# Order of TensorE inside an attention step: the products moved in front of the second pair's scores

## The chip, the cores and the metric

One core of a Trainium2 chip runs the whole kernel in one launch. The metric is the time on the device in microseconds (us), median of three runs. All inputs and outputs are 32-bit floats in device memory.

## The reference

An AdaLN block over x of shape (2, 1024, 256): causal attention with 32 query heads and 8 key/value heads of width 8, then a feed-forward layer with 16 routed experts (top 4) and a shared one. Cut to what matters here, the attention:

```python
q = (h @ wq) ; k = (h @ wk) ; v = (h @ wv)          # 32 query heads, 8 key/value heads, width 8
att = einsum('bhqd,bhkd->bhqk', q, k) / sqrt(8)
att = where(mask, -inf, att) ; att = softmax(att)    # causal, 1024 x 1024 per head
y = einsum('bhqk,bhkd->bhqd', att, v)
x = x + ga * (y @ wo)
```

## The kernel before

The kernel has a prologue (modulation, layer norm, projections), the attention core, a post stage (output projection, second norm, router) and the expert layer. The change is in the attention core alone.

**Groups and steps.** The core runs over 16 groups (2 batches times 8 key/value heads). A group holds four query heads, two "pairs of heads" hh = 0 and 1, and the two heads of a pair lie in the upper and lower 64 rows of the array (hp = 0, 1). The causal triangle of a group is cut into 12 steps (STEPS): queries in two halves of 512, keys in chunks c of 128. Steps 0 to 3 are the first half, steps 4 to 11 the second. Queries above the diagonal are left out, so the width of a step is 512, 384, 256, 128 in steps 0 to 3, 512 in steps 4 to 8, and 384, 256, 128 in steps 9 to 11. Below, step 8.6 is step 6 of group 8.

**The softmax needs the row maximum first.** While group g is worked on, TensorE also computes the scores of a later group in the other orientation (queries on partitions) and VectorE reduces them to maxima. These are the 12 wide units (`wide(n)`, into two PSUM banks that only they use, reduced by L709) and 12 narrow units (`narrow(n)`, one bank, reduced by L716) per group; step s of group g does unit n = 12(g+1) + 6 + s (AHEAD = 6). A next wide unit waits for `wide_free`, the end of the reduction before, a narrow one for `narrow_free`. The wide unit of step 6 is the first that reads the stacks (operands) of group g+2, and waits for their load (`stack_in`).

**One step.** `scores(group, s, hh)` writes two banks per pair of heads with keys on partitions (L665) and signals `st_full`; it may not start before ScalarE has read those banks for the step before (`p_full`). ScalarE takes one exponential per pair (L608, `probs<-psum`). `product(group, s)` (L679, `psum<-probs,v_aug`) multiplies the exponentials of all four heads with the values, four matmuls in four 32-column strips of the array (the profile counts eight, since a 32-bit float product runs as two passes), and adds into one bank, `sum_bank`. It runs LAG = 2 steps after its scores. On diagonal chunks GpSimd masks the exponentials first (L585).

**The sum bank.** Products 0 to 3 accumulate the first half, products 4 to 11 the second. When a half is complete, ScalarE copies the bank to `y_sb` (L600), queued behind both exponentials of step 5 (first half) and of step 1 of the next group (second half). The first product of a half waits for that copy:

```python
if c == 0 and 2 * group + half:
    pe.wait_ge(y_done, 2 * group + half)
```

With the lag of 2 these waiting products are product(4), issued in step 6, and product(0), issued in step 2.

**SyncE.** One queue issues all transfers. At the start of a group it waits until all scores of the group before are done, then issues the 16 loads of the stacks of group g+2 and, in groups 1 to 3, the three loads of an expert's raw weights:

```python
if 1 <= group < GROUPS - 2:
    sp.wait_ge(st_full, 2 * NSTEP * group)
    load_stacks(sp, group + 2)
```

In groups 0 to 3 ScalarE turns those raw weights into `w_hi` (L616), queued between the exponentials of step 3 and of step 4.

All engines run their instructions in the order written; only semaphores tie them together.

Of the kernel before, what the change touches and what calls it, by code (L numbers as in the profile page):

```python
# [31 lines left out]
GROUPS = B * NKV  # L32
# [34 lines left out]
NPAIR = len(WIDE)  # L67
# [19 lines left out]
def block_kernel(nc, x_in, wq_in, wk_in, wv_in, wo_in, wr_in, we1_in, we3_in, we2_in,  # L87
# [13 lines left out]
    with whole:  # L101
# [414 lines left out]
        with nc.Block() as block:  # L516
# [102 lines left out]
            @block.tensor  # L619
            def _(pe):  # L620
                def wide(n):

                    group = n // NPAIR
                    w, (h0, h1), tiles, chunk, _, diagonal = WIDE[n % NPAIR]
                    segments = [(hh, i) for hh in range(h0, h1) for i in range(*tiles)]
                    buf = group % NBUF
                    if n % NPAIR == 0:
                        pe.wait_ge(stack_in[buf], LOADS * (group // NBUF + 1))
                    if n:
                        pe.wait_ge(wide_free, n)  # L630
                    for k, (hh, i) in enumerate(segments):
                        key = i * P if w == P else chunk * P
                        for hp in range(2):
                            rows = slice(64 * hp, 64 * hp + 64)
                            if not diagonal:
                                keys = ku[buf][rows, key:key + w]
                            elif i % 4 == 0:
                                keys = kx[buf][rows, (i + 3) * P:(i + 4) * P]
                            else:
                                keys = (kx, kx, ky)[i % 4 - 1][buf][rows, key:key + w]  # L640
                            last = pe.matmul(bank[wide_bank + hp][:, k * w:(k + 1) * w], qs[buf][rows, hh, i * P:(i + 1) * P],  # L641
                                             keys, start=(k == 0), stop=(k == len(segments) - 1), skip_group_check=True)
                    last.then_inc(wide_full, 1)

                def narrow(n):

                    group = n // NPAIR
                    hp, hh, i = NARROW[n % NPAIR]
                    buf, rows = group % NBUF, slice(64 * hp, 64 * hp + 64)
                    if n:  # L650
                        pe.wait_ge(narrow_free, n)
                    pe.matmul(bank[narrow_bank][:], qs[buf][rows, hh, i * P:(i + 1) * P], ku[buf][rows, 0:TT],  # L652
                              start=True, stop=True).then_inc(narrow_full, 1)

                def scores(group, s, hh):

                    half, c, off = STEPS[s]
                    buf = group % NBUF
                    if s == 0 and hh == 0:
                        pe.wait_ge(row_in[buf], 32 * (group // NBUF + 1))  # L660
                    if 2 * NSTEP * group + 2 * s + hh > 1:
                        pe.wait_ge(p_full, 2 * NSTEP * group + 2 * s + hh - 1)
                    for hp in range(2):
                        rows = slice(64 * hp, 64 * hp + 64)
                        last = pe.matmul(bank[2 * hh + hp][:, off:TT], ks[buf][rows, c * P:(c + 1) * P],  # L665
                                         qs[buf][rows, hh, half * TT + off:(half + 1) * TT],
                                         start=True, stop=True)
                    last.then_inc(st_full, 1)

                def product(group, s):  # L670

                    half, c, off = STEPS[s]
                    if c == 0 and 2 * group + half:
                        pe.wait_ge(y_done, 2 * group + half)
                    pe.wait_ge(p_full, 2 * NSTEP * group + 2 * s + 2)
                    if c >= half * (TC // 2):
                        pe.wait_ge(p_masked, NDIAG * group + c + 1)
                    for h in range(REP):
                        last = pe.matmul(bank[sum_bank][32 * h:32 * h + 32, off:TT], v_aug[:, group, c, :],  # L679
                                         probs[:, s % (LAG + 1), h, off:TT], start=(c == 0),  # L680
                                         stop=(c == (TC // 2, TC)[half] - 1), skip_group_check=True)
                    last.then_inc(pv_done, 1)

                pe.wait_ge(parts_set, 1 + 2 * NBUF)
                for n in range(NPAIR + AHEAD):
                    wide(n)
                    narrow(n)
                for group in range(GROUPS):
                    for s in range(NSTEP):
                        n = NPAIR * (group + 1) + AHEAD + s  # L690
                        scores(group, s, 0)
                        if n < NPAIR * GROUPS:
                            wide(n)
                        scores(group, s, 1)
                        if n < NPAIR * GROUPS:
                            narrow(n)
                        if s >= LAG:
                            product(group, s - LAG)
                        elif group:
                            product(group - 1, s - LAG + NSTEP)  # L700
                for s in range(NSTEP - LAG, NSTEP):
                    product(GROUPS - 1, s)

            @block.vector
            def _(dve):
                def wide(n):
                    w, (h0, h1), tiles, _, slot, _ = WIDE[n % NPAIR]
                    dve.wait_ge(wide_full, n + 1)
                    dve.tensor_reduce(out=max_parts[:, :, h0:h1, slice(*tiles), slot],  # L709
                                      in_=psum[:, wide_bank:wide_bank + 2, :].rearrange("p a (s w) -> p (a s) w", w=w),  # L710
                                      axis=AX.X, op=ALU.max).then_inc(wide_free, 1)
# [438 lines left out]
```

## Time and profile before

| | us |
|---|---|
| median of three runs | 965.73 (963.19 to 966.53) |
| time of the profiled execution | 965.71 |
| its span | 963.8 |
| attention core (first scores to last product) | about 138.0 to 549 of the span |

Busy shares of the span: TensorE's matmuls 87%, its weight loads 56%, VectorE 68%, ScalarE 45%, GpSimd 21%. These are averages over stages with different limits; a matmul's end is modelled, so that matmuls that follow closely look like an engine that is always busy. Times below are in us from the span's start; a group of the core takes 24.1 us where nothing else disturbs it (groups 4 to 13), 30 to 32 us in groups 0 to 3, and about 22 us in the last two.

### The profile page before, as it was taken

The page shows a single profiled execution, that of the slowest core. Times are in us where ns is not written, and L with a number is a line of the kernel's source. Part 1 is how long each engine was busy: PE and PEld are TensorE (multiplying, and loading weights), DVE is VectorE, ACT ScalarE, POOL GpSimd, SP SyncE. Part 2 cuts the span into 40 slices and gives each one's busy share as a digit, 9 for nine tenths or more (in the row PEclk, how much of TensorE's full clock was granted, in tenths as well). Part 3 has the DMA queues.
Part 4 walks back from the last instruction along what each step waited for, and adds up shares of the span by engine and source line. Part 5 has one row for each costly group of instructions (what it writes and reads, how often), then busy time and mean ns, then how long its engine had stood idle before and what let it go on. Part 6 is the DMA issues. An engine that isn't in the chain of part 4 may idle for free. (4 is left out here: it accounts for less than half of the span.)

```text
span 963.8 us, 15004 instructions
## 1 busy us (share of the span) xinstructions
PE 835.8 (87%) x5472; PEld 539.3 (56%) x5472; DVE 659.6 (68%) x1053; ACT 433.0 (45%) x629; POOL 204.3 (21%) x261
## 2 busy tenths in 40 slices
PE   0791579879799999999999677699999999999996
PEld 0550334334344444444443257488888888888885
DVE  0751887678699999999994144777656666665665
ACT  3121016666677777777778704222222222222221
POOL 8600002122122222222222123782000000000000
PEclk9896558788899999999999976699999999999999
DMA  5069300443234343444430160440000000000000
GB/s 181 1 174 230 59 19 24 99 95 82 53 93 92 92 93 92 93 93 92 92 81 26 45 185 0 126 121 17 1 22 0 0 22 0 0 0 22 0 0 22
DMA packets 50627, 61.15 MB, mean 63 GB/s; under 512 B 12624, under 2 KB 37200, under 8 KB 49488
## 3 DMA queue, kind: packets, MB, share of 16 engines
q1 hardware_dynamic: 50576, 60.47, 25.6%
q8 instruction: 32, 0.52, 0.2%
q14 instruction: 19, 0.16, 0.1%
HBM read 42.35 MB, written 17.56 MB: 62 GB/s over the span
## 5 line engine op out<-in xcount | busy, mean ns | idle before, releaser
L608 ACT ACTIVATE probs<-psum 128x1024 f32<-128x1024 f32 (+3 forms) x384 | 289.0, 817 | 134.3 <-PE psum L665 132.3
L709 DVE TENSOR_REDUCE max_parts<-psum 128x8 f32<-128x1024 f32 (+2 forms) x192 | 235.0, 1224 | 58.6 <-PE psum L641 54.3
L665 PE MATMUL psum<-qs,ks 64*128 64x512 f32 (+3 forms) x768 | 162.4, 420 | 18.3 <-ACT probs L608 18.1
L679 PE MATMUL psum<-probs,v_aug 128*32 128x512 f32 (+3 forms) x1536 | 168.7, 513 | 0.3 <-POOL probs L585 0.2
L665 PEld LDWEIGHTS psum<-qs,ks 64*128 64x128 f32 x768 | 75.1, 192 | 154.5 <-ACT probs L608 132.8
L992 ACT ACTIVATE mid<-psum 128x512 f32<-128x512 f32 x80 | 47.9, 599 | 243.6 <-PE psum L1015 243.6
L585 POOL TENSOR_SCALAR_AFFINE_SELECT probs<-probs 128x512 f32<-128x512 f32 x128 | 81.4, 636 | 238.0 <-ACT probs L608 238.0
L716 DVE TENSOR_REDUCE max_parts<-psum 128x1 f32<-128x512 f32 x192 | 130.8, 681 | 0.0
L1103 DVE TENSOR_TENSOR mid<-mid,psum 128x512 f32<-128x512 f32 x80 | 54.9, 688 | 104.7 <-ACT mid L992 104.2
L1094 DVE SCALAR_TENSOR_TENSOR acc<-psum,cw,acc 128x256 f32<-128x256 f32 x240 | 99.2, 475 | 0.0
L652 PE MATMUL psum<-ku,qs 64*128 64x512 f32 x192 | 91.5, 476 | 0.0
L1015 PE MATMUL psum<-h_hi,wl_hi 128*128 x256 | 79.6, 392 | 0.0
L1015 PE MATMUL psum<-h_hi,wl_lo 128*128 x256 | 79.2, 390 | 0.0
L1015 PE MATMUL psum<-h_lo,wl_hi 128*128 x256 | 79.0, 390 | 0.0
L974 POOL TENSOR_TENSOR fin<-fin,gate 128x256 f32<-128x256 f32 x4 | 3.0, 738 | 294.3 <-DVE fin L1112 294.3
L679 PEld LDWEIGHTS psum<-probs,v_aug 128*32 128x32 f32 x1536 | 30.8, 109 | 58.2 <-issue 42.0
L641 PE MATMUL psum<-kx,qs 64*128 64x128 f32 (+1 forms) x384 | 38.9, 312 | 28.1 <-DVE ks L734 24.2
L1082 DVE TENSOR_TENSOR g_lo<-mid,g_hi 128x512 fp32r<-128x512 f32 x80 | 59.9, 749 | 1.0 <-ACT g_hi L988 0.9
L988 ACT ACTIVATE g_hi<-mid 128x512 fp32r<-128x512 f32 x80 | 50.0, 625 | 9.2 <-DVE mid L1103 7.8
L1015 PEld LDWEIGHTS psum<-h_hi,wl_lo 128*128 128x128 f32 x256 | 48.1, 188 | 10.6
L1015 PEld LDWEIGHTS psum<-h_lo,wl_hi 128*128 128x128 f32 x256 | 48.1, 188 | 10.4
L641 PEld LDWEIGHTS psum<-kx,qs 64*128 64x128 f32 x384 | 31.8, 212 | 36.4 <-DVE ks L734 24.3
(132 smaller groups left out, 1004.4 us busy)
## 6 DMA issues: line engine op xcount, KB each, us to landing
qs<-q_parts SPq DMA_DIRECT2D x64, 128.0 KB
y_sums<-y_sb SPq DMA_DIRECT2D x32, 256.0 KB, 3.0
wl_raw<-in_L_ffn_we_dram SPq DMA_DIRECT2D x36, 128.0 KB, 2.2
ks<-k_parts SPq DMA_DIRECT2D x32, 128.0 KB
ku<-k_parts SPq DMA_DIRECT2D x32, 128.0 KB
ky<-k_parts SPq DMA_DIRECT2D x32, 128.0 KB
kx<-k_parts SPq DMA_DIRECT2D x32, 96.0 KB
x_sb<-in_L_attn_x_dram SPq DMA_DIRECT2D x4, 512.0 KB, 7.6
```

The costliest lines, as they stand in the source:

```text
L585: pool.affine_select(out=tile, in_=tile, compare_op=ALU.is_ge, fill=0.0, base=0, pattern=[[0, REP], [1, P]], channel_multiplier=-1).then_i ...
L608: act.activation(probs[:, s % (LAG + 1), 2 * hh:2 * hh + 2, off:TT], psum[:, 2 * hh:2 * hh + 2, off:TT], ACT.Exp, scale=SCALE).then_inc(p_ ...
L641: last = pe.matmul(bank[wide_bank + hp][:, k * w:(k + 1) * w], qs[buf][rows, hh, i * P:(i + 1) * P], keys, start=(k == 0), stop=(k == len( ...
L652: pe.matmul(bank[narrow_bank][:], qs[buf][rows, hh, i * P:(i + 1) * P], ku[buf][rows, 0:TT], start=True, stop=True).then_inc(narrow_full, 1)
L665: last = pe.matmul(bank[2 * hh + hp][:, off:TT], ks[buf][rows, c * P:(c + 1) * P], qs[buf][rows, hh, half * TT + off:(half + 1) * TT], sta ...
L679: last = pe.matmul(bank[sum_bank][32 * h:32 * h + 32, off:TT], v_aug[:, group, c, :], probs[:, s % (LAG + 1), h, off:TT], start=(c == 0), ...
L709: dve.tensor_reduce(out=max_parts[:, :, h0:h1, slice(*tiles), slot], in_=psum[:, wide_bank:wide_bank + 2, :].rearrange("p a (s w) -> p (a ...
L716: dve.tensor_reduce(out=max_parts[:, hp, hh, i:i + 1, 1], in_=bank[narrow_bank][:], axis=AX.X, op=ALU.max).then_inc(narrow_free, 1)
L1015: last = pe.matmul(bank[2 * m + e % 2][:], w[:, col:col + H], h[:, c, bass.ds(at, TT)], start=(n == 0), stop=(n == 5))
L1082: dve.tensor_tensor(out=g_lo[:, e % 2, :], in0=mid[:, e % 2, :], in1=g_hi[:, e % 2, :].bitcast(F32), op=ALU.subtract).then_inc(glo_done, 1)
L1094: last = dve.scalar_tensor_tensor(out=acc[:, j, :], in0=y, scalar=weight, in1=acc[:, j, :], op0=ALU.mult, op1=ALU.add)
L1103: dve.tensor_tensor(out=m, in0=m, in1=bank[2 + e % 2][:], op=ALU.mult).then_inc(mult_done, 1)
```

## The change

The product of step s - 2 is issued directly behind the wide unit, ahead of the scores of the second pair of heads and of the narrow unit. No instruction is added or removed, and no wait is changed; no other engine's program changes.

```diff
@@ -691,13 +691,13 @@
                         scores(group, s, 0)
                         if n < NPAIR * GROUPS:
                             wide(n)
-                        scores(group, s, 1)
-                        if n < NPAIR * GROUPS:
-                            narrow(n)
                         if s >= LAG:
                             product(group, s - LAG)
                         elif group:
                             product(group - 1, s - LAG + NSTEP)
+                        scores(group, s, 1)
+                        if n < NPAIR * GROUPS:
+                            narrow(n)
```

TensorE's order in steps 5 and 6 of a group (the first rows are step 5). L665 are scores, L641 the wide unit, L652 the narrow one, L679 the product; the product of 128 columns is the last one of the first half, the product of 512 columns behind it the first of the second half. Before:

```order
L665 MATMUL psum<-qs,ks 128x512 x2
L641 MATMUL psum<-ky,qs 128x512 x2
L665 MATMUL psum<-qs,ks 128x512 x2
L652 MATMUL psum<-ku,qs 128x512
L679 MATMUL psum<-probs,v_aug 32x128 x4
L665 MATMUL psum<-qs,ks 128x512 x2
L641 MATMUL psum<-kx,qs 128x128 x8
L665 MATMUL psum<-qs,ks 128x512 x2
L652 MATMUL psum<-ku,qs 128x512
L679 MATMUL psum<-probs,v_aug 32x512 x4
```

and after:

```order
L665 MATMUL psum<-qs,ks 128x512 x2
L641 MATMUL psum<-ky,qs 128x512 x2
L679 MATMUL psum<-probs,v_aug 32x128 x4
L665 MATMUL psum<-qs,ks 128x512 x2
L652 MATMUL psum<-ku,qs 128x512
L665 MATMUL psum<-qs,ks 128x512 x2
L641 MATMUL psum<-kx,qs 128x128 x8
L679 MATMUL psum<-probs,v_aug 32x512 x4
L665 MATMUL psum<-qs,ks 128x512 x2
L652 MATMUL psum<-ku,qs 128x512
```

In step 6 the product that waits for the copy of the sum bank now stands ahead of the second pair's scores, and in step 5 the product that completes the bank too.

TensorE's order in step 11 and at the start of the next group, where the last scores of a group release SyncE's loads. Before:

```order
L665 MATMUL psum<-qs,ks 128x128 x2
L641 MATMUL psum<-ku,qs 128x512 x2
L665 MATMUL psum<-qs,ks 128x128 x2
L652 MATMUL psum<-ku,qs 128x512
L679 MATMUL psum<-probs,v_aug 32x384 x4
L665 MATMUL psum<-qs,ks 128x512 x2
```

and after:

```order
L665 MATMUL psum<-qs,ks 128x128 x2
L641 MATMUL psum<-ku,qs 128x512 x2
L679 MATMUL psum<-probs,v_aug 32x384 x4
L665 MATMUL psum<-qs,ks 128x128 x2
L652 MATMUL psum<-ku,qs 128x512
L665 MATMUL psum<-qs,ks 128x512 x2
```

A product of 384 columns now runs before the last scores of the group, where it ran behind them.

## Rows read from the trace of the kernel before

**Rows 1.** Page, part 1: busy us, share of the span, instructions of each engine.

```profile
PE 835.8 (87%) x5472; PEld 539.3 (56%) x5472; DVE 659.6 (68%) x1053; ACT 433.0 (45%) x629; POOL 204.3 (21%) x261
```

**Rows 2.** Windows: length, busy of PE, PEld, DVE, ACT, POOL, granted clock, DMA share, GB/s.

```profile
168.12:200.08 31.96, 27.69 (x204) 12.26 (x200) 22.33 (x27) 19.84 (x27) 7.36 (x12) 0.84 0.36 83
212.00:222.00 10.00, 7.18 (x38) 3.32 (x40) 4.11 (x6) 7.21 (x8) 2.28 (x3) 0.50 0.11 37
359.73:383.83 24.10, 24.00 (x205) 10.62 (x202) 22.22 (x27) 18.75 (x26) 5.55 (x11) 1.00 0.39 93
```

**Rows 3.** Timeline of steps 8.4 to 8.7: start, length, engine, line, operation.

```profile
367.45 0.49 PE L665 MATMUL psum<-qs,ks 64*128 64x512 f32 x2
...
368.04 1.94 ACT L608 ACTIVATE probs<-psum 128x1024 f32<-128x1024 f32 x2 [1.16 <-PE psum L665]
...
368.74 0.64 PE L679 MATMUL psum<-probs,v_aug 128*32 128x256 f32 x8
...
370.70 0.42 PE L679 MATMUL psum<-probs,v_aug 128*32 128x128 f32 x8
...
371.46 0.66 PE L641 MATMUL psum<-kx,qs 64*128 64x128 f32 x8
371.74 0.60 ACT L600 ACTIVATE y_sb<-psum 128x512 f32<-128x512 f32 x1
371.93 0.48 PE L665 MATMUL psum<-qs,ks 64*128 64x512 f32 x2
...
372.57 1.06 PE L679 MATMUL psum<-probs,v_aug 128*32 128x512 f32 x8
...
373.56 0.50 PE L665 MATMUL psum<-qs,ks 64*128 64x512 f32 x2
```

**Rows 4.** Timeline of steps 8.7 and 8.8, TensorE.

```profile
374.23 0.50 PE L665 MATMUL psum<-qs,ks 64*128 64x512 f32 x2
...
375.89 0.50 PE L665 MATMUL psum<-qs,ks 64*128 64x512 f32 x2
376.22 0.40 PE L641 MATMUL psum<-kx,qs 64*128 64x256 f32 x4
376.46 0.40 PE L665 MATMUL psum<-qs,ks 64*128 64x512 f32 x2
...
376.70 0.39 PE L652 MATMUL psum<-ku,qs 64*128 64x512 f32 x1
...
377.02 1.06 PE L679 MATMUL psum<-probs,v_aug 128*32 128x512 f32 x8
```

**Rows 5.** Waits in groups 4 to 13: who waited for whom, us in total, times, longest.

```profile
PEld psum L652 <- DVE max_parts L716: 8.7, 40, 0.3
...
PEld psum L641 <- DMA kx<-k_parts: 0.5, 2, 0.4
```

**Rows 6.** Timeline of steps 8.1 and 8.2, the other copy and its product.

```profile
363.53 0.63 ACT L600 ACTIVATE y_sb<-psum 128x512 f32<-128x512 f32 x1
...
364.78 1.07 PE L679 MATMUL psum<-probs,v_aug 128*32 128x512 f32 x8
```

**Rows 7.** Timeline of steps 14.6 and 14.7, without wide and narrow units.

```profile
516.34 0.60 ACT L600 ACTIVATE y_sb<-psum 128x512 f32<-128x512 f32 x1
...
516.99 1.06 PE L679 MATMUL psum<-probs,v_aug 128*32 128x512 f32 x8
...
518.83 0.49 PE L665 MATMUL psum<-qs,ks 64*128 64x512 f32 x2 [0.34 <-ACT probs L608]
519.25 0.64 PE L679 MATMUL psum<-probs,v_aug 128*32 128x512 f32 x4
```

**Rows 8.** Timeline of group 2 (its first scores start at 200.08).

```profile
199.00 0.77 SPq L188 DMA_DIRECT2D qs<-q_parts  x2
...
213.01 0.84 ACT L616 ACTIVATE w_hi<-w_raw 128x768 fp32r<-128x768 f32 x1 [5.75 <-DMA w_raw<-in_L_ffn_we_dram]
...
214.82 0.80 PE L665 MATMUL psum<-qs,ks 64*128 64x512 f32 x2 [5.06 <-ACT probs L608]
```

## The prediction

> **What bounds the kernel now.** I read the page first: TensorE's matmuls cover 87% of the span, more than any other engine [rows 1]. Since modelled ends hide short waits, I then cut the core into windows, one group each. An undisturbed group, such as group 8, takes 24.10 us, with TensorE busy for 24.00, VectorE for 22.22 and ScalarE for 18.75, all at full clock (1.00, the 2.4 GHz level) [rows 2]. So TensorE and VectorE are both close to their limit and ScalarE has slack on average. Groups 1 to 3 take about 32 us (group 1: 31.96) at a mean clock of 0.84 [rows 2]; what they wait for is in the timeline of group 2: ScalarE stands 5.75 us before `w_hi`, for the raw weights of an expert, and TensorE stands 5.06 us behind the exponential queued after it [rows 8]. Behind that gap the window 212 to 222 has a granted clock of 0.50, the 1.2 GHz level [rows 2].
>
> Inside a group the timeline shows what a step is made of. In step 8.8 nothing waits: scores to wide unit 376.22 - 375.89 = 0.33, wide to second scores 0.24, those to the narrow unit 0.24, narrow to product 0.32 [rows 4]; a product of 512 columns holds TensorE for 373.56 - 372.57 = 0.99 until the next scores start [rows 3]. The sum is 2.12 us. Step 8.7 is longer, 375.89 - 373.56 = 2.33, and 0.10 of it shows in wide to second scores: the latter start 0.67 behind the first scores (374.23) where 8.8 needs 0.57 [rows 3, 4]. They wait for the exponential of step 8.6. So ScalarE, idle on average, is the limit around steps 4 to 7 of each group, where all widths are 512 and the copy of the sum bank comes between.
>
> **The change part by part.** No instruction is added. TensorE's sum per step is the same if the two new neighbours cost what the old ones did. Wide to product: the rows have narrow to product at 0.32 [rows 4] and, without a wide unit between, a pair of scores to product at 519.25 - 518.83 = 0.42 [rows 7], the scores having waited; the lower bound is pair to pair, 0.24 [rows 4]. I take 0.32. Narrow to scores: I take 0.24, what pair to narrow costs; the upper bound is the 0.32 before a product. So 0.32 + 0.24 replaces 0.24 + 0.32, and the order is neutral by itself. What changes is who is ready when.
>
> *The second pair's scores come later*, by the length of the product. For 512 columns the timeline gives 1.06 with the modelled end and 0.99 to the next start; with the same 0.07 off, 256 columns take 0.64 - 0.07 = 0.57 and 128 take 0.42 - 0.07 = 0.35 [rows 3], and 384, halfway between 256 and 512, 0.78. *The product comes earlier*, ahead of scores and narrow unit. Its two waits for the copy of the sum bank are where both meet.
>
> Walk through steps 8.4 to 8.7, from the same start, 367.45. ScalarE's exponentials of 512 columns follow each other every 0.92 (two take 1.94, the second starting about 0.1 before the first ends) [rows 3].
> - Step 4: wide 367.45 + 0.33 = 367.78, product 368.10, second scores 368.10 + 0.57 = 368.67, complete 0.49 later at 369.16. The second exponential can start at 369.18; in the trace it started at 368.04 + 0.92 = 368.96. ScalarE is 0.22 late.
> - Step 5: scores 368.67 + 0.24 + 0.24 = 369.15, wide 369.49, product(3) 369.81, second scores 370.25, once the exponential of step 4 has ended at 370.20. Exponentials at 370.10 and 371.02, each 0.92 behind the former, the copy 371.94 to 372.54, where the trace has 371.74 to 372.34 [rows 3].
> - Step 6: the first scores wait for the first exponential of step 5, which ends at 371.12: 371.17. Eight small wide matmuls start later behind scores than two large ones, and I take 0.41: wide unit 371.58. The product would be ready 0.47 later (wide to scores, 371.93 - 371.46 [rows 3]), plus 0.08 as the difference of product to scores: 372.13. It waits for the copy, 372.54 + 0.05 = 372.59: **0.46 us of wait on TensorE**, with the second scores and the narrow unit queued behind it. They start at 373.58, where the trace has 371.93; the next step starts at 373.58 + 0.24 + 0.24 = 374.06 in place of 373.56: **+0.50**.
> - Step 7 then needs 2.13 and not 2.33, because its second scores no longer wait: **-0.19**.
>
> The same meeting at steps 1 and 2 is milder, and this walk is coarser. The copy runs 363.53 to 364.16 and product(0) starts 364.78 [rows 6]. With the second scores of step 1 pushed back by 0.35 less the wait they had, the copy ends near 364.47, product(0) starts at 364.52, the narrow unit follows at 364.52 + 1.0 + 0.12, and step 3 starts near 365.9 in place of 365.78 (364.78 + 1.00): **+0.15**. On the other side the narrow units wait for their bank: 8.7 us of idle weight-load queue in 40 waits, 0.87 us a group, of which only the part in steps bound by TensorE comes back [rows 5]. With the product ahead of it the narrow unit finds its bank free; I count the one wait of about 0.1 in step 11, **-0.1**. An undisturbed group becomes 0.50 - 0.19 + 0.15 - 0.1 = 0.36 us longer.
>
> *VectorE* gets the narrow unit later: wide to narrow becomes 0.32 + 1.0 + 0.24 = 1.56 in place of 0.48, and its wide reduction is done 1.14 after its start, so it idles ahead of the narrow one and no longer ahead of the wide one. The next wide unit is complete 0.24 + 0.33 + 0.40 - 0.39 = 0.58 behind the narrow one, while the narrow reduction takes 0.68: 0.1 late, which nobody waits for. Cost 0.
>
> *SyncE* is moved too. Its loads are released by the last scores of a group. In the trace the first load goes out at 199.00, 1.08 ahead of the next group's start [rows 8]. Behind a product of 384 columns (0.78), they complete about 0.2 ahead of it. Everything on that queue starts 0.9 later in its group. In groups 1 to 3 the raw weights are the bound: `w_hi` starts 213.01 - 200.08 = 12.93 into group 2, and all of step 5 hangs on it [rows 8]. So each becomes **+0.9** longer, less the 0.1 of step 11: 0.8. The waits for the copy cost nothing there, the first hidden under the stall of 5.06, the second because at the 0.50 clock wide unit and product are slower than the copy. From group 4 on only the stacks are loaded, and they arrive barely in time: in two groups of ten the wide unit of step 6 already waited, 0.5 us together [rows 5]. If that wait grows, it falls ahead of product(4), which waits 0.46 anyway, so I count 0 and keep 0.3 per group for the upper end.
>
> *The last two groups* have no wide unit and ScalarE runs without a pause. In step 14.6 product(4) starts at 516.99, as soon as the copy has ended (516.94) [rows 7]. Now the second scores stand behind it: 517.99, complete 518.48; their exponential would have followed the copy and one exponential, 516.84 + 0.92 = 517.76. That is +0.74 on the engine that bounds this stretch, and again in group 15; with about 0.25 for each of the two other places: **+2.0**.
>
> **Sum.** Groups 4 to 13: 10 x 0.36 = 3.6. Groups 1 to 3: 3 x 0.8 = 2.4. Group 0: 0.2. Groups 14 and 15: 2.0. Together +8.2 on the profiled execution's 965.71, which is the median of the runs (965.73) within 0.02: **974 us**. The post stage and the experts follow unchanged.
>
> **The rivals.**
> 1. *The product drains more behind a pair of matmuls* (slower still). Wide to product costs the 0.42 of the pair in rows 7 and not 0.32. Seven steps a group (2, 6 to 11) have no other limit, so 0.7 x about 13 = +9 more: 983. For it: the only row of a pair ahead of a product. Against it: those scores had waited, and step 8.7, where wide to second scores took 0.34 (0.67 less 0.33) after a wait, shows that a start that waited costs about 0.1 by itself [rows 4]. The Trainium skill, TensorEngine Tiling (Array Packing), Key Properties, says that a change of tiling mode drains the array. By that rule the change from 64-row to 32-column tiles costs the same twice a step in both orders, and only what is drained differs; the 0.32 behind one narrow matmul agrees with a drain but no row shows the wide one. Chance 0.17.
> 2. *No change.* Wide to product costs only 0.24, as between pairs. Then 7 x 0.08 = 0.56 a group comes back, 14 x 0.56 = 7.8, and the sum ends at +0.4: 966. Against it: every product in the trace starts at least 0.3 behind what precedes it. Chance 0.12.
> 3. *Faster: the copy is not what product(4) waits for.* The point that decides is 0.46 us: if the sum bank's copy ends before 372.13 on the clock of step 8.6, the +0.50 and +0.15 vanish, and what stays is the relief of second scores and narrow units, between -0.29 and -(0.19 + 0.87) a group. With -0.4, near the small end, over 13 groups and +2.4 for groups 1 to 3: -2.8, 963. For it: product(3) is out 0.89 earlier (370.70 to 369.81), so its own end never delays the copy. Against it: the copy is queued behind two exponentials that cannot be earlier. Chance 0.08.
> 4. *The forecast*, both kinds of copy wait and the later release of SyncE: 974, its own range 970 to 979. Chance 0.63.
>
> **How the numbers follow.** What a measurement of this kernel can tell from no change is about 0.3%, 2.9 us. Cases 1 and 4 are slower (0.80), case 2 within it and, with a small share of the edges, 0.12; case 3 faster, 0.08. The range runs from 967, between cases 2 and 4, to 984, past case 1, where it takes in 0.3 a group for the stacks. About 0.1 is left out on either side, nearly all of it below.
>
> **What would show it.** In the changed profile: an undisturbed group of 24.4 to 24.6 us; in the waits, product L679 held by `y_sb` L600 in every group for about 0.5; in steps 4 and 5 the second exponential later, and step 7 at 2.13; `w_hi` starting 13.8 us into groups 1 to 3; step 14.6 with product at about 517 and second scores at 518. It would be wrong if wide to product is far from 0.32, if the start that waits adds its own 0.1 behind a late product, or if the later release makes the wide unit of step 6 wait longer than the copy does.

## The result and the profile after

The changed kernel takes 978.78 us (978.27 to 981.78, 4 runs) against 964.46 us (962.42 to 966.53, 4 runs) of the kernel before: a ratio of 1.0155, 95% interval 1.0122 to 1.0188. It is slower by 1.2 to 1.9%. The forecast was slower, 974, with a range of 967 to 984. The sign and the place are right; the size is off. Between the two medians lie 14.3 us where I had summed 8.2.

First the windows of the changed kernel, groups 1, 2, 3, 8, 14, 15 and two short stretches (columns as in [rows 2]):

```profile
166.64:199.68 33.04, 27.94 (x202) 12.97 (x204) 22.61 (x27) 20.08 (x27) 7.37 (x11) 0.85 0.34 80
199.68:233.74 34.06, 27.95 (x204) 12.96 (x204) 22.60 (x27) 20.06 (x27) 7.37 (x11) 0.80 0.39 77
233.74:265.72 31.98, 26.88 (x202) 12.80 (x204) 22.50 (x27) 20.07 (x27) 7.38 (x11) 0.84 0.35 82
365.40:390.32 24.92, 23.81 (x202) 11.08 (x204) 22.32 (x27) 19.23 (x26) 5.56 (x10) 1.00 0.37 89
514.86:538.54 23.68, 21.70 (x175) 8.62 (x176) 12.60 (x16) 19.12 (x26) 5.27 (x10) 1.00 0.08 26
538.54:563.49 24.95, 20.86 (x162) 6.71 (x160) 1.75 (x1) 19.21 (x27) 6.02 (x10) 0.93 0.10 33
543.20:546.60 3.40, 3.40 (x20) 0.75 (x17) 0.00 (x0) 1.16 (x3) 0.40 (x2) 0.54 0.21 77
214.00:225.00 11.00, 9.20 (x50) 4.71 (x50) 5.27 (x7) 8.04 (x9) 2.28 (x3) 0.50 0.10 30
```

The undisturbed group went from 24.10 [rows 2] to 24.92 us, while TensorE's busy time in it went down, 24.00 to 23.81: it does the same work and waits more. All of the loss is in the attention core. The first scores start at 137.76 (before 138.04) and the last product ends at 563.49 (before 549.44), and what follows takes 413.6 us (before 414.4).

The waits in groups 4 to 13, the counterpart of [rows 5]:

```profile
DVE max_parts L716 <- PE psum L652: 21.8, 50, 0.8
PEld psum L641 <- DVE max_parts L709: 18.5, 60, 0.4
...
PEld psum L679 <- ACT y_sb L600: 9.5, 19, 0.7
...
PE psum L679 <- ACT y_sb L600: 6.0, 18, 0.5
PEld psum L641 <- DMA kx<-k_parts: 2.2, 6, 0.6
```

The product now waits for the copy of the sum bank, 0.5 at most on the matmul side, as forecast. Two further lines are larger than I gave them credit for: VectorE stands before the narrow reduction (21.8 us in 50 waits), and the wide unit stands for the end of the wide reduction (60 waits, six in each of ten groups).

Steps 8.3 to 8.6 of the changed kernel, the counterpart of [rows 3]:

```profile
372.82 1.22 DVE L709 TENSOR_REDUCE max_parts<-psum 128x4 f32<-128x1024 f32 x1
...
374.10 0.50 PE L641 MATMUL psum<-ky,qs 64*128 64x512 f32 x2
...
374.53 0.64 PE L679 MATMUL psum<-probs,v_aug 128*32 128x256 f32 x8
...
375.64 2.85 ACT L608 ACTIVATE probs<-psum 128x1024 f32<-128x1024 f32 x3 [0.44 <-PE psum L665]
...
377.63 0.50 PE L665 MATMUL psum<-qs,ks 64*128 64x512 f32 x2 [0.18 <-ACT probs L608]
...
377.98 0.56 PE L641 MATMUL psum<-kx,qs 64*128 64x128 f32 x8
378.37 0.61 ACT L600 ACTIVATE y_sb<-psum 128x512 f32<-128x512 f32 x1
...
379.04 1.06 PE L679 MATMUL psum<-probs,v_aug 128*32 128x512 f32 x8 [0.51 <-ACT y_sb L600]
...
380.04 0.50 PE L665 MATMUL psum<-qs,ks 64*128 64x512 f32 x2
```

Read upwards from the product at 379.04: it idled 0.51 for the copy (378.37 + 0.61 = 378.98). The copy followed three exponentials, the second of step 4 and both of step 5, that started at 375.64 after ScalarE had stood 0.44 for scores. Those were late because the wide unit of step 4 started only at 374.10: it waited for the wide reduction of step 3, which ran from 372.82 to 374.04. So one delay feeds the next, from VectorE through ScalarE to the product. Where the delay at VectorE comes from, and what it is worth, is taken up behind the experiments.

### The profile page after: what moved, and what is told of

It reads as the page before. It is cut to its first block and busy times, and to the rows that moved or that the text cites. A ratio compares the mean times of both kernels' runs of the same rounds, so it can differ in the third digit from the quotient of the medians.

```text
span 977.1 us, 15004 instructions
## 1 busy us (share of the span) xinstructions
PE 835.9 (86%) x5472; PEld 546.0 (56%) x5472; DVE 660.3 (68%) x1053; ACT 439.5 (45%) x629; POOL 204.7 (21%) x261
## 5 line engine op out<-in xcount | busy, mean ns | idle before, releaser
L608 ACT ACTIVATE probs<-psum 128x1024 f32<-128x1024 f32 (+3 forms) x384 | 295.8, 811 | 143.2 <-PE psum L665 143.0
L709 DVE TENSOR_REDUCE max_parts<-psum 128x8 f32<-128x1024 f32 (+2 forms) x192 | 234.2, 1220 | 26.0 <-PE psum L641 24.7
L665 PE MATMUL psum<-qs,ks 64*128 64x512 f32 (+3 forms) x768 | 171.5, 421 | 19.4 <-ACT probs L608 18.6
L679 PE MATMUL psum<-probs,v_aug 128*32 128x512 f32 (+3 forms) x1536 | 171.2, 519 | 11.1 <-ACT y_sb L600 10.3
L665 PEld LDWEIGHTS psum<-qs,ks 64*128 64x128 f32 x768 | 82.9, 192 | 163.1 <-ACT probs L608 139.5
L652 PE MATMUL psum<-ku,qs 64*128 64x512 f32 x192 | 86.1, 448 | 0.0
L641 PE MATMUL psum<-kx,qs 64*128 64x128 f32 (+1 forms) x384 | 44.5, 310 | 28.3 <-DVE ks L734 23.9
L679 PEld LDWEIGHTS psum<-probs,v_aug 128*32 128x32 f32 x1536 | 30.8, 109 | 51.0 <-issue 23.7
L641 PEld LDWEIGHTS psum<-kx,qs 64*128 64x128 f32 x384 | 37.6, 211 | 37.9 <-DVE ks L734 24.1
```

What stands on the lines that cost most here:

```text
L608: act.activation(probs[:, s % (LAG + 1), 2 * hh:2 * hh + 2, off:TT], psum[:, 2 * hh:2 * hh + 2, off:TT], ACT.Exp, scale=SCALE).then_inc(p_ ...
```

## The experiments

The theories at the outset:
- *Copy*: the product that waits for the copy of the sum bank holds up the second scores (and what follows from that).
- *VectorE*: the late narrow unit costs by itself, through VectorE and the wide bank.
- *SyncE*: the last scores of a group release the loads later.

All runs were compared with the kernel before on the same chip. "Group" means an undisturbed one of groups 4 to 13.

**1. Only the narrow unit behind the product.**

```diff
-                        if n < NPAIR * GROUPS:
-                            narrow(n)
                         if s >= LAG:
                             product(group, s - LAG)
                         elif group:
                             product(group - 1, s - LAG + NSTEP)
+                        if n < NPAIR * GROUPS:
+                            narrow(n)
```

> Order of a step: first scores, wide unit, second scores, product, narrow unit. Only the narrow unit is behind the product; the second scores stand where they stood before the change. If the waits for the copy of the sum bank are the whole loss (copy theory), nothing stands behind them but the narrow unit: an undisturbed group stays near 24.1 us, the kernel within 2 us of before. If VectorE's late narrow reductions, which then hold the wide bank, are a part of it (VectorE theory), a group takes 24.4 us or more and the kernel is 4 to 7 us slower than before. SyncE's release is as before in both, so groups 1 to 3 keep their 31.3 to 32 us.

Measured: 964.81 us, ratio 0.9997 (0.9978 to 1.0016), a group of 24.07 us. The wide unit waits for VectorE here too (21.6 us in 60 waits, more than in the changed kernel), but a late narrow unit alone costs nothing; the VectorE theory falls as a cause of its own. Groups 1 to 3 take 31.0, 32.5 and 31.6 us, two of them outside the 31.3 to 32 expected though SyncE's release is as before, so half a microsecond in a single one of these groups says little.

**2. Only the second scores behind the product.**

```diff
                             wide(n)
-                        scores(group, s, 1)
                         if n < NPAIR * GROUPS:
                             narrow(n)
                         if s >= LAG:
                             product(group, s - LAG)
                         elif group:
                             product(group - 1, s - LAG + NSTEP)
+                        scores(group, s, 1)
```

> Order of a step: first scores, wide unit, narrow unit, product, second scores. Only the second scores are behind the product. Copy theory: the product still waits for the copy ahead of the second scores, so nearly the whole loss stays, a group of 24.7 to 25 us and 976 to 980 us in all. VectorE theory: the narrow unit is early, VectorE has no gap, and at least 0.3 us a group comes back against the changed kernel, 24.6 us or less, near 973 us. SyncE's loads are released even later, so groups 1 to 3 are no shorter than in the changed kernel.

Measured: 989.03 us, ratio 1.0233 (1.0214 to 1.0253), a group of 25.5 us, 0.6 more than in the changed kernel. The expectation of the VectorE theory is missed by 0.9 us a group, but that of the copy theory is missed as well, by 0.5 us a group and 9 us in all. With the narrow unit early, the second scores start even later (in step 8.8 1.90 behind the first ones, in the changed kernel 1.72). Most of the extra 0.6 lies in steps 4 and 8 to 11, and not in the two steps of the copy; why each of those is longer isn't shown. The run rules out that an early narrow unit repairs the loss, and no more.

**3. The old order in the two steps of the copy.** A flag chooses, per step, where the product stands; here and in runs 4, 6, 7 and 8 only its condition differs:

```diff
+                        early = s not in (LAG, TC // 2 + LAG)
+                        if early:
+                            late_product()
                         scores(group, s, 1)
                         if n < NPAIR * GROUPS:
                             narrow(n)
+                        if not early:
+                            late_product()
```

> The changed order in all steps but 2 and 6, the two whose product waits for the copy; those keep the order of before. Copy theory: the waits of product L679 for y_sb vanish, a group takes 24.1 to 24.3 us, the last two groups 22.6 each, and what is left over before is the later release of SyncE in groups 1 to 3 (about 3 us): 967 to 970 us. VectorE theory: the narrow unit is still late in ten of twelve steps, so a group keeps at least 24.5 us and the kernel 972 us or more.

Measured: 973.12 us, ratio 1.0073 (1.0044 to 1.0102). About half of the loss is gone, but the groups are unequal, 24.25 to 25.01 us. The waits tell why (groups 4 to 13):

```profile
PEld psum L641 <- DMA kx<-k_parts: 5.6, 9, 1.0
...
PE psum L641 <- DMA kx<-k_parts: 3.0, 7, 0.7
```

With the copy's wait gone, the wide unit of step 6 waits for the stacks, up to 1.0 us. In the changed kernel that wait had been hidden ahead of the copy's. The copy theory's numbers (24.1 to 24.3 us a group, 967 to 970) are both missed. VectorE's total (972 or more) is met, its 24.5 us a group is not met in three of the ten groups. Run 3 alone can't separate them, runs 5 and 11 do.

**4. The old order in step 11 alone** (condition `early = s != NSTEP - 1`).

> The changed order in all steps but 11, which keeps the order of before, so that the last scores of a group, and with them SyncE's loads, are not behind a product. SyncE theory (0.9 us in each of groups 1 to 3 comes from the later release): raw weights land about 13 us into the group and not 14, groups 1 to 3 are 0.7 to 1 us shorter each than in the changed kernel, 976 us in all, and a group from 4 on stays at 24.9. If the release doesn't matter: groups 1 to 3 as in the changed kernel (33.0, 34.1, 32.0), 978 to 979 us.

Measured: 981.54 us, ratio 1.0156 (1.0137 to 1.0175). Groups 1 to 3 take 30.7, 31.1 and 32.6 us in place of 33.0, 34.1 and 32.0, together 4.7 less, and `w_hi` starts 12.60 us into group 2 in place of 14.30: the later release is real. The kernel gets no faster and misses its 976, since a group takes 25.22 us, 0.3 more, and group 15 takes 27.4 us with two stretches at half clock in it. Step 11 takes 2.38 us where it took 1.74; the two steps behind it give back 0.33. In a step of the old order behind one of the new, the second scores stand early again, but the exponential that must have read their banks is still late: that of step 8.10 ends at 387.84, and the second scores of step 8.11 start at 387.89. I had not foreseen this cost of mixing.

**5. The copy between the two exponentials** (TensorE in the changed order).

```diff
                                            psum[:, 2 * hh:2 * hh + 2, off:TT], ACT.Exp, scale=SCALE).then_inc(p_full, 1)
-                        if s == 1 and group:
-                            sums(group - 1, 1)
-                        if s == 5:
-                            sums(group, 0)
+                            if hh == 0 and s == 1 and group:
+                                sums(group - 1, 1)
+                            if hh == 0 and s == 5:
+                                sums(group, 0)
```

> The changed order on TensorE, and ScalarE copies the sum bank between the two exponentials of steps 1 and 5 and not behind both, so that the copy ends about 0.9 us earlier in its step. If the wait of the first product of a half for the copy is a main part of the loss, the waits of L679 for y_sb shrink to near 0 and an undisturbed group drops from 24.92 to 24.5 us or less, 972 to 974 us in all. Rival (ScalarE's chain of exponentials is late by itself, whatever waits for the copy): the copy only moves the second exponential of steps 1 and 5 back by 0.5 us, the group stays at 24.8 to 25 us.

Measured: 969.83 us, ratio 1.0050 (1.0028 to 1.0072). That is below the 972 to 974 expected. No wait for `y_sb` is left in the table of waits. Two windows, groups 4 and 7:

```profile
264.15:288.16 24.01, 23.71 (x202) 11.03 (x204) 22.31 (x27) 19.14 (x26) 5.54 (x10) 1.00 0.36 94
...
336.95:361.45 24.50, 23.94 (x202) 11.07 (x204) 22.42 (x27) 19.13 (x26) 5.54 (x10) 1.00 0.42 91
```

A group without a stack wait takes 24.01 us, below the 24.10 of before. The rival, that ScalarE's chain is late whatever waits for the copy, falls.

**6. The new order only in the two steps of the copy** (condition `early = s in (LAG, TC // 2 + LAG)`).

> The order of before in all steps but 2 and 6, which take the changed order. The product that waits for the copy is ahead of the second scores, but no other product is, and SyncE's release is as before. Copy theory: the copy ends as early as before (372.3 in group 8), product(4) could start 372.1, so the wait is only 0.2, yet the second scores of step 6 still follow the product; group 24.3 to 24.6 us, 968 to 972 us in all. If the later second scores of all other steps are the loss: 24.1 us, within 2 us of before.

Measured: 984.22 us (979.04 to 986.91; the profiled execution 979.04), ratio 1.0208 (1.0181 to 1.0236), a group of 25.22 us. Steps 3 and 7, each behind one of the new order, take 2.37 and 2.93 us where they took 1.67 and 2.32 before; with the steps ahead of them, the pairs 2 and 3 are 0.35 longer and the pairs 6 and 7 0.74. In step 8.7 the second scores stand 0.42 for the exponential of the step before. Both expectations miss: the cost of mixing, met in run 4, is larger here than what was to be measured. The run shows that this cost exists in a step of 512 columns too; it can't tell it from the copy's wait (0.28 in step 8.6).

**7. The new order only in steps 7 to 10** (condition `early = 7 <= s <= 10`).

> The changed order only in steps 7 to 10, where the changed kernel's steps were no longer than before (7: 2.19 against 2.32, 9: 1.94 against 2.06, 8 and 10 equal). If these gains stand by themselves, a group becomes 23.85 to 24.0 us and the kernel 1 to 3 us faster than before. If they only gave back what earlier steps had lost, a group stays at 24.1 us or gets longer, because step 11 has to make up for the product that moved (2.38 against 1.79 in the run with step 11 alone in the old order).

Measured: 970.18 us, ratio 1.0045 (1.0027 to 1.0063), a group of 24.3 us, step 11 at 2.39. The shorter steps were paid back in the next one. There is no gain to pick out of the changed order step by step.

**8. The old order in steps 2, 6 and 11** (condition `early = s not in (LAG, TC // 2 + LAG, NSTEP - 1)`).

> The order of before in steps 2, 6 and 11, the changed one elsewhere. In the run with the old order at steps 2 and 6 alone, groups varied from 24.25 to 25.01 us and the wide unit waited for stacks for 8.6 us in ten groups. With step 11 in the old order too, SyncE's release is early again: if those waits come from the later release, the stack waits fall below 1 us and the groups are equal within 0.1 us, at 24.3 to 24.6 us; groups 1 to 3 take 31.5 us or less each. If they don't, the spread of 0.7 us stays.

Measured: 969.44 us, ratio 1.0053 (1.0032 to 1.0073). All ten groups take 24.55 to 24.57 us and no wait for stacks is left; groups 1 to 3 take 30.9, 32.6 and 30.3. So the spread in run 3 came from the later release. A group is still 0.45 above the old order's 24.10 though no product waits for the copy on the matmul side. Runs 4, 6 and 7 make mixing the likely reason, since run 11 below, which changes all steps alike, doesn't have it; no run takes the 0.45 apart. Of the three groups 1 to 3 one missed its 31.5.

**9 to 12. The loads out of the way.** SyncE issues an expert's weights, and of the stacks the key tiles that only the wide and narrow units read, ahead of its wait for the last scores. The same edit was put on four kernels:

```diff
                 for group in range(GROUPS):
-                    if 1 <= group < GROUPS - 2:
-                        sp.wait_ge(st_full, 2 * NSTEP * group)
-                        load_stacks(sp, group + 2)
                     if group < NEARLY:
                         if group >= 2:
                             sp.wait_ge(lo2, group - 1)
                         load_expert(sp, w_raw[:, group % 2, :], we1_in[group], we3_in[group], we2_in[group], raw_in[group % 2])
+                    if 1 <= group < GROUPS - 2:
+                        sp.wait_ge(wide_free, NPAIR * group)
+                        sp.wait_ge(narrow_free, NPAIR * group)
+                        load_keys(sp, group + 2)
+                        sp.wait_ge(st_full, 2 * NSTEP * group)
+                        load_scored(sp, group + 2)
```

`load_keys` holds the eight transfers of ku, ky and kx, `load_scored` the eight of qs and ks.

> The order of before on TensorE. SyncE issues an expert's raw weights ahead of its wait for the last scores of a group, and of the stacks it loads ku, ky and kx (eight of sixteen transfers, read only by the wide and narrow units) ahead of that wait too; only qs and ks stay behind it. If the wait for the last scores is what makes w_hi late in groups 1 to 3, the waits of w_hi for w_raw vanish, the granted clock stays at 1.00 there, groups 1 to 3 take 24.5 to 26 us in place of 31.3 to 32.0, and the kernel is 17 to 22 us faster than before. If the transfers themselves are the limit, groups 1 to 3 stay over 29 us. Groups 4 to 13 stay at 24.1 us in both cases.

> The changed order on TensorE with the same early loads. SyncE's part of the loss is taken away, the copy's is not: groups from 4 on stay at 24.9 us (their stack waits had been hidden ahead of the wait for the copy), groups 1 to 3 become about 25.5 to 26.5 us. Against the kernel with the order of before and early loads it is 11 to 15 us slower, 0.8 us in each of 13 to 14 groups and the last two. If stack waits had been a visible part of the 24.9, the group falls to 24.6 us or less.

> The changed order, the copy between the two exponentials of steps 1 and 5, and the early loads. If copy and SyncE's release are together the whole loss, every group from 4 to 13 takes 24.0 us (as the groups without a stack wait did, 24.01), spread below 0.1 us, the wide unit waits for no stacks, and the kernel is within 2 us of the order of before with early loads, or up to 2 us faster. If the order has a cost of its own, groups stay at 24.3 us or more.

> First scores, wide unit, second scores, product, narrow unit, with the early loads. Without stack waits the group was 24.05 us with this order (24.10 with the order of before), so I expect a kernel within 1.5 us of the order of before with early loads. It tells again whether a late narrow unit costs anything when loads are out of the way: over 24.3 us a group it does.

| order on TensorE, with early loads | us | ratio to before (95%) | groups 1 to 3 | groups 4 to 13 | 14, 15 |
|---|---|---|---|---|---|
| 9: as before | 944.04 | 0.9758 (0.9716 to 0.9800) | 24.10 | 24.09 to 24.11 | 22.6, 24.7 |
| 10: changed | 956.97 | 0.9905 (0.9875 to 0.9935) | 24.92 to 24.95 | 24.90 to 24.93 | 23.7, 23.7 |
| 11: changed, copy between | 939.18 | 0.9730 (0.9689 to 0.9771) | 24.00 to 24.01 | 23.98 to 24.05 | 22.6, 22.3 |
| 12: narrow unit behind product | 942.06 | 0.9747 (0.9709 to 0.9785) | 24.07 to 24.08 | 24.05 to 24.08 | 22.8, 22.6 |

The windows of group 1 and group 8 in run 10, the changed order:

```profile
166.63:191.55 24.92, 23.79 (x202) 10.99 (x204) 22.32 (x27) 19.85 (x27) 7.36 (x11) 1.00 0.37 103
...
341.08:365.99 24.91, 23.80 (x202) 11.06 (x204) 22.31 (x27) 19.23 (x26) 5.53 (x10) 1.00 0.35 89
```

and in run 11, with the copy between the exponentials:

```profile
166.16:190.17 24.01, 23.70 (x202) 10.98 (x204) 22.32 (x27) 19.75 (x27) 7.39 (x11) 1.00 0.39 106
...
334.23:358.21 23.98, 23.68 (x202) 11.00 (x204) 22.30 (x27) 19.13 (x26) 5.56 (x10) 1.00 0.36 93
```

With the loads early, group 1 takes what group 8 takes, at full clock, in each of the four. The stall of 5 us of groups 1 to 3 was SyncE's order, not the transfers. The changed order keeps its 24.9 us: the loads had no part in that number. And moving the copy by one exponential takes 0.92 us out of each group and ends 0.1 us below the old order. So the copy's wait, with what hangs on it, is the whole cost of the change in an undisturbed group. Its waits in groups 4 to 13, run 10:

```profile
DVE max_parts L730 <- PE psum L666: 22.5, 50, 0.8
PEld psum L655 <- DVE max_parts L723: 18.5, 60, 0.5
...
PEld psum L693 <- ACT y_sb L614: 11.5, 20, 0.7
...
PE psum L693 <- ACT y_sb L614: 8.1, 20, 0.5
```

and run 11:

```profile
PEld psum L655 <- DVE max_parts L723: 18.4, 60, 0.4
...
DVE max_parts L730 <- PE psum L666: 13.5, 50, 0.4
```

(L655 is the wide unit here, L666 the narrow one, L693 the product.) The 60 waits of the wide unit are as long in both, 18.5 and 18.4 us, so they don't carry the copy's wait, and in run 11 they cost the group nothing. What goes is the product's wait for `y_sb` and 9.0 us of VectorE's standing before the narrow reduction. By steps, all that group 8 gains from run 10 to run 11 lies in the two places of the copy: step 2 goes from 2.51 to 2.14 us, steps 6 and 7 from 4.93 to 4.35, and no other step moves by more than 0.03. Run 11 is the version that beats both kernels: 939.2 us, 2.7% below before, and further below run 9 than the 2 us expected. Its lead over run 9 (4.9 us between medians, 6.5 between the profiled executions' spans) is not all its order: 1.0 us of the 6.5 are the ten groups and 0.3 groups 1 to 3, while 2.4 lie in group 15 and 2.5 in group 0, in both of which run 9 was longer at low clock. The old order with the copy moved was not run, so whether the 0.1 us a group belongs to the order or to the place of the copy isn't shown. Runs 9 and 10 are 12.9 us apart, inside the 11 to 15 expected; groups 1 to 3 came out shorter than expected in both, and run 12 is 2.0 us faster than run 9 where I had allowed 1.5.

## Why the prediction was right in sign and short in size

**The sum per step.** It held. Step 8.8 takes 2.13 us in both kernels, where I had 2.12. Wide to product measured 0.43 in steps 0, 4, 5, 10 and 11 (374.53 - 374.10 in step 8.4) and 0.39 in step 8.8, where I took 0.32 and rival 1 took 0.42. Second scores to narrow unit took 0.34 where I had 0.24, and both came back behind the narrow unit, where the next scores start 0.07 later and not 0.24 (last section). So rival 1 had the number nearly right and its consequence (+9 us) wrong. The Trainium skill (TensorEngine Tiling (Array Packing), Key Properties) lets the array drain at a change of tiling mode. The 0.43 behind a pair of 512 columns, against the 0.32 behind a single matmul of that width, agrees with that. But a wide unit of the same form (four matmuls of 256 columns) has 0.39 in step 8.8 of the changed kernel and 0.32 in step 8.7 of run 11 (348.76 to 349.08), and no run measures the drain alone.

**The wait of product(4) for the copy.** Forecast 0.46, measured 0.51. The second scores at 380.04, 1.00 behind it, are as drawn.

**What leads up to it.** This is the term that was mis-sized. I had steps 4 to 7 together at +0.31 (0.50 - 0.19); they take 9.16 in place of 8.43, +0.73. Steps 0 to 3 were put at +0.15 and take 8.01 in place of 7.72, +0.29. Steps 8 to 11 give back 0.17, where I had 0.1. The group's +0.36 is thus +0.82.

The sentence that fails is that on VectorE, "0.1 late, which nobody waits for. Cost 0". The wide unit of step 4 is what waits. In the changed kernel (group 8):

```profile
373.40 0.44 PE L652 MATMUL psum<-ku,qs 64*128 64x512 f32 x1
...
374.09 0.19 PEld L641 LDWEIGHTS psum<-ky,qs 64*128 64x128 f32 x2 [0.45 <-DVE max_parts L709]
```

It comes 0.69 behind the narrow unit, where the walk has 0.24 + 0.33 = 0.57, and its product follows after 0.43 and not 0.32. The second scores, and the exponentials behind them, are later by both. Counted from the later of the two first scores, steps 4 and 5 take 3.94 (373.69 to 377.63) where the walk has 3.72 (367.45 to 371.17). Most of the rest of the miss is the coarse walk of steps 1 and 2.

This delay is not handed on by the copy's wait in step 2. In run 11 no product waits for the copy, and the same place of group 8 reads

```profile
341.87 0.44 PE L666 MATMUL psum<-ku,qs 64*128 64x512 f32 x1
...
342.56 0.18 PEld L655 LDWEIGHTS psum<-ky,qs 64*128 64x128 f32 x2 [0.45 <-DVE max_parts L723]
```

with the same 0.69 and the same wait of 0.45; steps 4 and 5 take 3.95 there (342.15 to 346.10). It comes with the narrow unit behind the product: VectorE needs about 1.9 us a step for its two reductions (1.22 and 0.68), and steps 3 to 5 of the old order were only 1.67, 1.86 and 1.74 long. By itself it costs the group nothing, as runs 1 and 11 show. Run 11 makes up for it in steps 6 and 7, which take 4.35 where the old order took 4.83. In the changed kernel product(4) stands for the copy just there, and they take 4.93. So both waits for the copy are the cause, and what the sum missed is that they meet a TensorE, and a ScalarE, that are later than drawn.

**SyncE.** The mechanism was right and the size short. The timeline of group 2 of the changed kernel (start 199.68), the counterpart of [rows 8]:

```profile
199.88 0.77 SPq L188 DMA_DIRECT2D qs<-q_parts  x2
...
213.98 0.84 ACT L616 ACTIVATE w_hi<-w_raw 128x768 fp32r<-128x768 f32 x1 [5.71 <-DMA w_raw<-in_L_ffn_we_dram]
...
215.79 0.80 PE L665 MATMUL psum<-qs,ks 64*128 64x512 f32 x2 [5.69 <-ACT probs L608]
```

The first load goes out 0.20 behind the group's start, where it went out 1.08 ahead and I had it 0.2 ahead; `w_hi` starts 14.30 into the group, in place of 12.93 (+1.37, forecast +0.9). Groups 1 to 3 took 1.1, 2.1 and 0.7 us more, 3.9 together against 2.4. Run 1, with the release of before, is off by -0.9, +0.6 and +0.3 in them, so the start of `w_hi` and the sum say more than a single group. Group 2's extra is the clock: its stretch at half clock lasted 13.65 us by the record of the clock where it was 10.24 before, and step 7, which had been back at full clock, took 3.54 in place of 2.30. Group 0 went the other way, 28.9 in place of 30.1, since its low clock ended earlier (150.4 in place of 153.9); no step of mine spoke of that, and the runs don't tie it to the change.

**The last groups.** Forecast +2.0, measured +1.1 and +2.4. Of group 15's, about 1.3 is a stretch that I had not thought of: product(0) idled 0.81 for the copy up to 543.05, the granted clock was 0.54 for 3.4 us (window 543.20 to 546.60), near the 1.2 GHz level, and that product took 1.94 where it takes 1.06:

```profile
543.05 1.94 PE L679 MATMUL psum<-probs,v_aug 128*32 128x512 f32 x8 [0.81 <-ACT y_sb L600]
```

The runs don't tie this stretch to the change. Run 10 has the same wait of 0.81 there (at 518.82), keeps full clock, and takes 23.7 us for group 15; run 9, in the old order, has a granted clock of 0.50 for 6.8 us in its group 15 (508.12 to 514.95) and takes 24.7.

**Sum.** Groups 4 to 13: 10 x 0.82 = 8.2 (forecast 3.6). Groups 1 to 3: 3.9 (2.4). Groups 14 and 15: 3.5 (2.0). Group 0: -1.2 (+0.2). Together 14.4; the core went from 549.44 - 138.04 = 411.4 to 563.49 - 137.76 = 425.7 us, +14.3.

**The rivals.** Nothing of the no-change case is left, since wide to product never fell to 0.24 (at least 0.36 in groups 4 to 13). Rival 3 named the point that decides, a copy that ends before the product is ready; the change didn't reach it, and run 11 did, by moving the copy: there 0.1 us a group is gained on the old order, not the 0.3 to 1.1 that I gave it, and the place of the copy may have a part in it.

That the total fell inside the range is in part the width of the range, opened to 984 for rival 1 and for stack waits, and neither of these is what filled it. The -1.2 of group 0 and the +1.3 within group 15, which no run ties to the change, happen to cancel.

## What to carry to other kernels

A wait in an in-order queue costs what stands behind it, so before moving work, ask which instruction of the group carries the long wait and what it is moved ahead of. Moving the awaited work (here a copy of 0.6 us, one place forward in ScalarE's queue) may be worth more than the order that is being tuned. A walk through a tight place must also follow the engines that look idle: here VectorE was called 0.1 late and free, and it held the unit ahead of the product in every group; that costs nothing until a wait stands where the time would have been made up. And a queue of transfers released by the last step of a group should carry ahead of that release all that doesn't need it: here that was 22 us (966.20 to 944.04), more than the 14.3 of the change.

## What was not expected of the hardware

A narrow unit uses one half of the array's rows, and the scores that now follow it start beside it. The timeline of TensorE in run 11 (there L666 is the narrow unit, L679 the scores, L655 the wide unit):

```profile
343.90 0.39 PE L666 MATMUL psum<-ku,qs 64*128 64x512 f32 x1
343.91 0.62 PE L679 MATMUL psum<-qs,ks 64*128 64x512 f32 x2
344.39 0.50 PE L655 MATMUL psum<-ky,qs 64*128 64x512 f32 x2
```

One of the two scores starts 0.01 behind the narrow unit (I took 0.24), and the wide unit follows 0.49 behind it, near the 0.24 + 0.33 of the old steps, so the sum stays. In the changed kernel (375.44 and 375.68) the scores that start at once are those in the rows that this narrow unit doesn't use, and those in its own rows start 0.24 later. A start-to-start gap of neighbours is thus no price by itself when they use different rows.

The other is the clock in group 15 of the changed kernel: waits of under a microsecond each, in a stretch where TensorE was busy for 1.82 of the 3.2 us ahead of it (540.0 to 543.2), were followed by 3.4 us at near half clock; in groups 4 to 13, with TensorE at 23.8 of 24.9 us, nothing of the kind was seen. It isn't sure to follow either: the same waits in run 10 left the clock at full speed.
